# Three full attentions in one kernel: weighted values and denominators interleaved, projections moved between the two score passes

## The reference, cut to what matters

```
qh = (LN(x) @ Wq.T + bq)   kh = (ctx @ Wk.T + bk)   vh = (ctx @ Wv.T + bv)     16 heads of 16
scores = (qh . kh) * tau[b] + delta[b, key]                                    per block: 128 x 128 per head
out    = softmax(scores / 4) @ vh, then @ Wo.T + bo, added to x
```

## Time and profile before

| | |
|---|---|
| median of 3 runs | 3175.97 us (3165.88 to 3178.23) |
| profiled execution, its own time | 3181.17 us |
| its span, first to last instruction | 3179.4 us |
| mean granted TensorE clock | 0.979 of full |
| PE / PEld / DVE / ACT / POOL busy | 3012.5 / 2218.9 / 2170.3 / 1117.8 / 891.5 us |

### The profile page before, as it was taken

One profiled execution on the slowest core, in us unless ns is written; L12 is line 12 of the kernel. 1 busy time (PEld: TensorE's weight loads), 2 busy tenths in 40 slices (PEclk: granted clock), 3 DMA queues, 4 the chain that ended last, 5 costly groups with the idle time before them and its releaser, 6 DMA issues. The chain is left out here.

```text
span 3179.4 us, 65748 instructions
## 1 busy us (share of the span) xinstructions
PE 3012.5 (95%) x27018; PEld 2218.9 (70%) x27034; DVE 2170.3 (68%) x6079; ACT 1117.8 (35%) x1963; POOL 891.5 (28%) x921
## 2 busy tenths in 40 slices
PE   8998999999899979888999999999999978998999
PEld 6676766566567656667888888888888866666444
DVE  5666345111366689666899989998999984666666
ACT  5654221222356679544222222222222204554000
POOL 2322000233232222001444444444444541332000
PEclk9999999999999999998999999999999979999999
DMA  4000220243400000402000000000000001000000
GB/s 150 29 29 16 62 77 21 72 119 93 133 29 29 15 12 1 146 24 80 5 5 6 5 5 5 5 6 5 5 4 6 5 31 68 29 28 2 14 20 20
DMA packets 79242, 112.36 MB, mean 35 GB/s; under 512 B 11872, under 2 KB 62304, under 8 KB 78560
## 3 DMA queue, kind: packets, MB, share of 16 engines
q1 hardware_dynamic: 71760, 98.58, 9.3%
q0 software_dynamic: 6144, 8.52, 1.4%
q10 hardware_dynamic: 1040, 1.05, 0.1%
HBM read 87.03 MB, written 21.10 MB: 34 GB/s over the span
## 5 line engine op out<-in xcount | busy, mean ns | idle before, releaser
L2194 POOL TENSOR_TENSOR pk_hisig<-pk_hihot,pk_sigs 128x512 f16<-128x512 f16 x512 | 520.4, 1043 | 664.9 <-DVE pk_hihot L2470 663.4
L2292 PE MATMUL pk_ps<-X,dw_downT 128*128 128x256 f32 x2048 | 480.5, 385 | 0.0
L2338 PE MATMUL pk_ps<-ew_up,pk_act_h 128*128 128x256 f32 x2048 | 461.5, 384 | 1.7 <-DVE pk_act_h L2458 1.7
L2338 PEld LDWEIGHTS pk_ps<-ew_up,pk_act_h 128*128 128x128 f32 x2048 | 390.5, 192 | 57.7 <-issue 2.0
L2292 PEld LDWEIGHTS pk_ps<-X,dw_downT 128*128 128x128 f32 x2048 | 381.1, 191 | 60.1 <-issue 14.8
L2202 ACT ACTIVATE pk_act_h<-pk_ps 128x512 f32<-128x512 f32 x256 | 153.0, 598 | 546.4 <-PE pk_ps L2292 546.4
L668 DVE TENSOR_REDUCE a_mx<-a_ps_s 128x8 f32<-128x1024 f32 x192 | 226.3, 1221 | 148.9 <-PE a_ps_s L499 134.2
L2471 DVE TENSOR_TENSOR pk_lohot<-pk_iota_h,pk_ps 128x1024 f16<-128x1024 f16 x256 | 310.4, 1213 | 0.0
L681 DVE RECIPROCAL a_rden<-a_ps_o 128x256 f32<-128x256 f32 x96 | 168.7, 1757 | 145.2 <-PE a_ps_o L550 145.2
L340 ACT ACTIVATE a_pT<-a_ps_s 128x512 f32<-128x512 f32 x384 | 198.3, 602 | 127.1 <-PE a_ps_s L516 127.1
L2672 PE MATMUL mo_ps<-mw_we,mo_xnT 128*128 128x512 f32 x512 | 224.5, 595 | 0.0
(11 more groups left out here) (380 smaller groups left out, 5199.4 us busy)
## 6 DMA issues: line engine op xcount, KB each, us to landing
ro_w<-in_L_W SPq DMA_DIRECT2D x16, 1024.0 KB, 7.4
i_ctx_t<-in_ctxT SPq DMA_DIRECT2D x16, 512.0 KB, 3.9
i_side<-in_side SPq DMA_DIRECT2D x16, 512.0 KB, 4.8
row_dram<-sh_row SPq DMA_DIRECT2D x8, 512.0 KB, 3.0
sum_dram<-sh_new SPq DMA_DIRECT2D x8, 512.0 KB, 2.9
X<-sum_dram SPq DMA_DIRECT2D x4, 1024.0 KB, 9.5
wa_ctx_t<-in_ctxT SPq DMA_DIRECT2D x8, 512.0 KB, 3.9
dw_downT<-in_L_downT SPq DMA_DIRECT2D x1, 4096.0 KB, 14.0
```

The costliest lines, as they stand in the source:

```text
L2194: ins = pool.tensor_tensor(hisig[:, buf, n, :, :, :], hi, sig2.broadcast_to([P, TP, 2, ECH]), ALU.mult)
L2292: ins = pe.matmul(hid.bank(f"h{c}")[:, j * 2 * P:(j + 1) * 2 * P], downT[:, k, e * P:(e + 1) * P], XT[:, p, k, :], start=(k == 0), stop=(k ...
L2338: ins = pe.matmul(tail.bank("y")[:, 0:D], act_h[:, p % 2, c, s * P:(s + 1) * P], up[:, c, :], start=(c == 0), stop=(c == ECH - 1))
```

## The change

```
--- before.py
+++ after.py
@@ -347,21 +347,23 @@
 
             def first_filler(g, u):
                 s, m = g % 2, ps_m[:, :]
-                if u == 0:
+                if u == 0 and g + 1 < GROUPS:
+                    queries(g + 1, 1 - s, 0, m)
+                elif u == 1 and g + 1 < GROUPS:
+                    keys(g + 1, 0, m)
+                elif u >= 2 and g + 2 < GROUPS:
+                    columns(g + 2, u - 2, m)
+
+            def second_filler(g, u):
+                s, m = g % 2, ps_m[:, :]
+                if u == 0 and g + 1 < GROUPS:
+                    queries(g + 1, 1 - s, 1, m)
+                elif u == 1 and g + 1 < GROUPS:
+                    keys(g + 1, 1, m)
+                elif u == 2:
                     values(g, s, 1, m)
-                elif u == 1 and g + 1 < GROUPS:
-                    queries(g + 1, 1 - s, 0, m)
-                elif u == 2 and g + 1 < GROUPS:
-                    queries(g + 1, 1 - s, 1, m)
                 elif u == 3 and g + 1 < GROUPS:
                     values(g + 1, 1 - s, 0, m)
-
-            def second_filler(g, u):
-                m = ps_m[:, :]
-                if u < 2 and g + 1 < GROUPS:
-                    keys(g + 1, u, m)
-                elif u >= 2 and g + 2 < GROUPS:
-                    columns(g + 2, u - 2, m)
 
             def tile(g, u):
                 t = g * G + u
@@ -430,10 +432,12 @@
 
             def tile(g, u):
                 t = g * G + u
-                if g + 1 < GROUPS and u in (1, 2):
-                    keys(g + 1, u - 1)
+                if g + 1 < GROUPS and u == 2:
+                    keys(g + 1, 1)
                 if t >= 3:
                     rows(t - 3)
+                if g + 1 < GROUPS and u == 1:
+                    keys(g + 1, 0)
 
             if arrival and arrival.scatter:
                 arrival.scatter(pool)
@@ -526,7 +530,7 @@
                     ins = pe.transpose(ps_z[:, f * P:(f + 1) * P], mx_flat[:, lo:lo + P], ident[:, :])
                 ins.then_inc(z_full, 1)
 
-            def weighted_values(t):
+            def values_and_sums(t):
                 g, u = t // G, t % G
                 s = g % 2
                 pe.wait_ge(p_taken, 4 * t + 4)
@@ -536,17 +540,12 @@
                     pe.wait_ge(v_taken, 2 * g + u // 2 + 1)
                 for c in range(KC):
                     for e in range(2):
+                        half = e * DK
                         for r in range(4):
-                            half = e * DK
                             pe.matmul(ps_o[32 * r:32 * r + 32, c * P:(c + 1) * P],
                                       v[:, s, u * HEADS // 2 + 4 * c + r, half:half + 32], pT[:, 4 * r + 2 * c + 1 - e, :],
                                       start=(c == 0 and e == 0), stop=(e == 1), skip_group_check=True)
-
-            def denominators(t):
-                for c in range(KC):
-                    for e in range(2):
                         for r in range(4):
-                            half = e * DK
                             ins = pe.matmul(ps_o[32 * r:32 * r + 32, D + c * P:D + (c + 1) * P],
                                             ones[:, half:half + 32], pT[:, 4 * r + 2 * c + 1 - e, :],
                                             start=False, stop=(e == 1), skip_group_check=True)
@@ -564,52 +563,53 @@
                 pe.wait_ge(xt_taken, g * 2 + n + 1)
 
             def first_filler(g, u):
-                s, m, more = g % 2, ps_m[:, :], g + 1 < GROUPS
-                if u == 0:
+                m, more = ps_m[:, :], g + 1 < GROUPS
+                if u == 0 and more:
                     if g == 0:
                         columns_taken(0, 1)
+                    else:
+                        pe.wait_ge(v_taken, 2 * g + 1)
+                    queries(g + 1, 0, m)
+                elif u == 1 and more:
+                    pe.wait_ge(q_taken, (g + 1) * KC + 2)
+                    keys(g + 1, (g + 1) % 2, 0, m)
+                elif u == 2 and g + 2 < GROUPS:
+                    pe.wait_ge(k_taken, (g + 1) * KC + 2)
+                    columns(g + 2, 0, m)
+                elif u == 3 and g + 2 < GROUPS:
+                    pe.wait_ge(v_taken, 2 * g + 2)
+                    columns(g + 2, 1, m)
+
+            def second_filler(g, u):
+                s, m, more = g % 2, ps_m[:, :], g + 1 < GROUPS
+                if u == 0 and more:
+                    pe.wait_ge(q_taken, (g + 1) * KC + 1)
+                    queries(g + 1, 1, m)
+                elif u == 1 and more:
+                    pe.wait_ge(k_taken, (g + 1) * KC + 1)
+                    keys(g + 1, 1 - s, 1, m)
+                elif u == 2:
+                    if g + 2 < GROUPS:
+                        columns_taken(g + 2, 0)
                     elif more:
-                        columns_taken(g + 1, 1)
+                        pe.wait_ge(k_taken, (g + 1) * KC + 2)
                     else:
                         pe.wait_ge(v_taken, 2 * g + 1)
                     values(s, 1, m)
-                elif u == 1 and more:
-                    pe.wait_ge(k_taken, (g + 1) * KC + 1)
-                    queries(g + 1, 0, m)
-                elif u == 2 and more:
-                    pe.wait_ge(k_taken, (g + 1) * KC + 2)
-                    queries(g + 1, 1, m)
                 elif u == 3 and more:
                     if g + 2 < GROUPS:
-                        columns_taken(g + 2, 0)
+                        columns_taken(g + 2, 1)
                     else:
-                        pe.wait_ge(q_taken, (g + 1) * KC + 2)
+                        pe.wait_ge(v_taken, 2 * g + 2)
                     values(1 - s, 0, m)
-
-            def second_filler(g, u):
-                s, m = g % 2, ps_m[:, :]
-                if u == 0 and g + 1 < GROUPS:
-                    pe.wait_ge(v_taken, 2 * g + 2)
-                    keys(g + 1, 1 - s, 0, m)
-                elif u == 1 and g + 1 < GROUPS:
-                    pe.wait_ge(q_taken, (g + 1) * KC + 1)
-                    keys(g + 1, 1 - s, 1, m)
-                elif u == 2 and g + 2 < GROUPS:
-                    pe.wait_ge(q_taken, (g + 1) * KC + 2)
-                    columns(g + 2, 0, m)
-                elif u == 3 and g + 2 < GROUPS:
-                    pe.wait_ge(v_taken, 2 * (g + 1) + 1)
-                    columns(g + 2, 1, m)
 
             def tile(g, u):
                 t = g * G + u
                 if t + 1 < TILES:
                     scores(t + 1)
                 if t:
-                    weighted_values(t - 1)
+                    values_and_sums(t - 1)
                 first_filler(g, u)
-                if t:
-                    denominators(t - 1)
                 turned_scores(t)
                 if t + 1 < TILES:
                     if integers and t == TOTALS_AT + 1:
@@ -653,8 +653,7 @@
                 if t == 1:
                     columns_taken(1, 1)
                 tile(t // G, t % G)
-            weighted_values(TILES - 1)
-            denominators(TILES - 1)
+            values_and_sums(TILES - 1)
             for t in (TILES - 2, TILES - 1):
                 output_rows(t)
 
```

## The result

The changed kernel takes 3156.39 us (median, 3154.73 to 3158.02, 4 runs) against 3175.68 (3165.88 to 3178.23, 4 runs): ratio 0.9942, 95% interval 0.9927 to 0.9956, 19.3 us faster by the medians. Forecast were 3155.0 and 21.0.

The account below looks back on a forecast made before the run. Attention tiles were taken as bound by TensorE (u = 0, 1) or a three-engine loop (u = 2, 3). Groups 1 to 5 give -4.80, edges -0.48, -1.00, -0.71: 6.99 per attention, 21.0 for three, 3155.0 us; range 3142 to 3169.

Parts of the forecast that it names:

- What bounds a tile: Attention tiles before the change: TensorE itself in u = 0 and 1 (9.09); a three-engine loop in u = 2 and 3 (8.39).
- One stretch: Weighted values and denominators back to back: 1.88 instead of 2.02, 0.14 saved; interleaving taken at nothing, bound 0.7 per tile.
- u = 0 and 1: These tiles: second filler waits 0.34 for the copy out of `ps_m`; 9.29 each, 0.18 and 0.20 more than before.
- u = 2 and 3: These tiles: turned scores at 3.67, no wait of next scores for exponentials; 7.73 each, a gain of 0.67.
- GpSimd and DVE: Keys' first product on GpSimd behind rows of t-3, and DVE's division, cost nothing; without cover, delayed maxima paid in u = 2.
- Edges: First and last groups of an attention: tile 0 +0.72, tile 1 +0.14, group 0 -0.48, group 6 -1.00, last group -0.71.
- The sum: One attention gains 6.99, three gain 21.0: 3175.97 to 3155.0 us, 0.66%.
- stages outside that move: Sign against the prediction: it is wrong if the stages outside the attentions move; no size given.
- the bank isn't waited for: Rival, u = 0 and 1 of groups 1 to 6: no 0.34 wait, 12.2 more gained, 3143; chance 0.12.
- the maxima take the place: Rival, u = 2 and 3: DVE's maxima late for turned scores; 0.34 late costs 14.3, 3169; chance 0.16.
- interleaving breaks the rotation: Rival, joint stretch: 14 added alternations in each of 96 stretches slow it; at 53 ns each 3226; chance 0.06.

Follow-up runs that it names:

- e1: The kernel before with only the joint interleaved stretch of weighted values and denominators, projections dealt as before: 3171.36 us, ratio to before 0.9993.
- e4: The changed kernel with the one stretch as 16 matmuls of values, then 16 of denominators, not interleaved: 3155.95 us, ratio to before 0.9944.
- e8: The changed kernel with one more activation out of `ps_m` ahead of the copy of queries(g+1,0), in u = 0: 3167.13 us, ratio to before 0.9979.
- e2: The changed kernel with weighted values and denominators apart again, around the first filler: 3146.13 us, ratio to before 0.9915.
- e3: The changed kernel with GpSimd's former order, keys product ahead of rows(t-3) in u = 1: 3165.03 us, ratio to before 0.9969.
- e5: The changed kernel's new dealing, denominators apart from weighted values only in u = 0 and 1, one stretch elsewhere: 3143.05 us, ratio to before 0.9906.

## Why the prediction was right

Point by point, by its own steps:

- *What bounds a tile* was right for each of the four kinds of tile, and e1 bears it out: shortening TensorE's work by 0.14 in each tile moves the group by 0.02, since in u = 2 the loop over ScalarE stands on the queries' copy and in u = 1 the bank does.
- *One stretch*: 1.88 forecast, 1.89 measured; interleaving at nothing, shown by e4. The count behind its bounds was wrong: 32 records are 16 matmuls, so the trace shows eight blocks of four matmuls and thus seven alternations where the unmixed stretch has one. That is 6 more in a tile and 576 in all, not 14 and 1344, and four matmuls take 0.20 us, not 0.10. At half of that per alternation the bound is 0.6 in a tile, not 0.7, and the rival would have eaten the gain at 36 ns each, not 16. Measured is 0.01 on the whole stretch.
- *u = 0 and 1*: 9.29 forecast, 9.29 measured. The wait was put at 0.34, and the second filler comes 1.61 behind the turned scores (115.04 to 116.65) instead of 1.27; the row shows 0.30 of it as waiting. e8 shows that it has no slack, e2 that the denominators had covered it. The Trainium skill's *TensorEngine Tiling (Array Packing)*, section "Performance Considerations", says that tiling speeds up TensorE but not the emptying of PSUM, which may then become the bottleneck; the trace shows such a hold for this one bank, with 0.30 in 14 tiles of an attention, brought about here by the order and not by more tiling.
- *u = 2 and 3*: 7.73 forecast, 7.72 measured, turned scores at 3.65 for 3.67.
- *GpSimd and DVE*: costed at nothing, with the price if the cover were gone. e3 took it away and paid 0.49 in each u = 2 tile, 1.5 where DVE had more to do.
- *Edges*: the last group -0.71 forecast and measured. Tile 1 was put at 8.57 and came at 8.49. Tile 0 was put at 9.55, 0.72 more, and came at 9.69, 8.07 and 9.69. The 8.84 it was worked out from was itself taken at a granted clock of 0.81 in all three attentions. At full clock the former filler gives 7.23 (e1) and the new one 8.07, so tile 0 costs 0.84 to 0.85 at either clock, and the 8.07 is the luck of a faster clock.
- *Missed*: tile 8 in layers 0 and 1. The table load there had ended 0.25 ahead of the turned scores; with the queries' copy in front of it, it ends at 108.01 and the exponentials start at 108.03. The prediction saw this in tile 0 and not in tile 8. It is worth 0.6 twice, and tiles 2 and 3, 6 and 7 of these layers are 0.05 longer than forecast.
- *The sum*: 21.0 forecast, 21.3 in the attentions' tiles, 19.3 between medians. That 21.0 and 21.3 agree so closely is in part luck. Behind tile 0 the forecast was 23.1 (21.0 and three times 0.72), and 22.3 was measured; the two tiles 8 alone cost 1.2. Against that, one tile 0 in the profile ran at full clock and took 1.6 less than the other two; without it the tiles would have gained 19.7, which is near the medians' 19.3. The 1.9 that the span gained outside the tiles was not forecast, and the prediction had named stages outside that move as a sign against it. The stage that moved runs the same code in all the kernels of the table, and with the change it lies within the range of the other eight, so it doesn't bear on the mechanism.

Of the rivals, "the bank isn't waited for" is refuted by the row of 0.30, "the maxima take the place" holds only if GpSimd's order is left as it was, and "interleaving breaks the rotation" is refuted by the stretch of 1.89, the same in e4. The rule set beside that last one, from the Trainium skill's *TensorE: Matmul & The Clock Gate*, "Part 3: Packing small matmuls" (a weight load overlaps matmuls only in other row groups), would have exposed loads; the trace disagrees: 64 loads, all on the same rows, pass within 1.89 in either order.

The change is thus two changes. Dealing the projections anew, with GpSimd's product behind the rows, is worth some 29 us in the tiles (10.9 would be lost with GpSimd's former order, as e3 shows in the changed kernel). Joining the stretch takes 6.5 of them back, because it removes the cover over a copy; by the tiles of e5, it is worth having only where the copy is short, and there 1.8.

## What to carry to other kernels

Write a tile as two sums, the work of the busiest engine and the loop through the shared banks, and take the larger for each kind of tile; a saving in the smaller one is worth nothing, and in e1 a saving of 0.14 was even paid back elsewhere. Work that stands between producing into a single bank and producing into it again is cover for its copy: before merging or moving it, compare the copy's end with the next writer, here 3.48 after the filler's start. Put the long filler where the loop leaves the array idle, and the short one inside the loop.

## What the runs showed of the hardware beyond that

Tile 0 takes one of a few lengths with the same program. Two windows of the changed kernel, tile 0 in layers 0 and 1:

```profile
33.00:38.00 5.00, 5.00 (x60) 2.98 (x56) 2.57 (x3) 0.83 (x2) 0.00 (x0) 0.68 0.01 2
...
846.20:850.00 3.80, 3.24 (x42) 1.75 (x40) 3.05 (x3) 1.16 (x2) 0.00 (x0) 1.00 0.02 4
```

The granted clock is 0.68 over the one and 1.00 over the other, that is partly the 1.2 GHz level in the first and 2.4 GHz throughout the second, after the same two waits for ScalarE's normalisation, with the weight loads idle for 1.53 and 0.57 us in the one and 1.54 and 0.56 in the other. The tile takes 9.69 and 8.07. In nine of the ten kernels of the table the same tile came out differently in the three attentions, by up to 1.6 (in the tenth, the kernel before, it took 8.84 three times). By an estimate from this, three times 1.6, up to 4.9 us of the difference between two executions can lie there. What decides which level is granted isn't shown by these runs.
